# Sparse attention with a two-deep exp arena, context products issued one head pair late, and V passed through device memory

## The reference

```python
x = x + layernorm(attention(layernorm(x)))      # block-sparse, 64 blocks of 64 tokens
x = x + layernorm(ffn(layernorm(x)))            # silu(x Wg) * (x Wu), then Wd; hidden 3072
# attention: query block qb attends to key blocks
#   0 and 63 : all 64
#   1        : 0, 1, 2, 63         62 : 0, 61, 62, 63
#   others   : 0, qb-1, qb, qb+1, 63
# each: softmax(q k^T / 8) v
```

## Time and profile before

| | us |
|---|---|
| median of 3 runs | 2392.13 (2385.08 to 2399.96) |
| profiled execution, its own time | 2390.2 |
| span of its slowest core (core 1) | 2388.7 |
| spans of all cores | 2375.0 to 2388.7 |
| `_p2`, from PE's first score matmul to its last context matmul | 491.6 to 897.5 |

### The profile page before, as it was taken

One profiled execution on the slowest core, in us unless ns is written; L12 is line 12 of the kernel. 1 busy time (PEld: TensorE's weight loads), 2 busy tenths in 40 slices (PEclk: granted clock), 3 DMA queues, 4 the chain that ended last, 5 costly groups with the idle time before them and its releaser, 6 DMA issues.

```text
span 2388.7 us, 31359 instructions; the slowest of 8 cores (2375.0 to 2388.7 us)
## 1 busy us (share of the span) xinstructions
PE 1660.0 (69%) x11234; PEld 802.9 (34%) x11234; DVE 850.9 (36%) x2276; ACT 587.5 (25%) x794; POOL 339.1 (14%) x510
## 2 busy tenths in 40 slices
PE   0069999977777770000002989999999989999994
PEld 0024444444444440000001434444444434444442
DVE  3514343344444446466671111223122131223123
ACT  2421111155665441212222101112111111112121
POOL 2011212202111211000001202111111212121110
PEclk9999999977666765555556999999999999999997
DMA  9933323311112128985638717655656758665653
GB/s 230 276 93 71 82 60 89 123 47 63 55 55 87 33 45 177 206 186 135 151 106 163 75 19 71 120 57 91 86 57 120 71 107 78 117 60 99 78 66 104
DMA packets 359497, 239.33 MB, mean 100 GB/s; under 512 B 313008, under 2 KB 314672, under 8 KB 357296
## 3 DMA queue, kind: packets, MB, share of 16 engines
q0 software_dynamic: 225456, 111.33, 33.1%
q1 hardware_dynamic: 120064, 92.43, 15.7%
q10 hardware_dynamic: 13824, 33.56, 4.2%
HBM read 205.53 MB, written 75.63 MB: 118 GB/s over the span
## 4 chain that ended last, share of the span: by engine, by line
PE 43%; DVE 7%; DMA 6%; SPq 3%; ACT 2%; issue 1%; ACTq 1%; DVEq 0%; POOL 0%; POOLq 0%
PE gp L913 14%; PE upp L919 14%; PE yp L931 7%; DMA xn_d<-p_xn 4%; PE upp L931 3%; PE gp L931 3%; SPq L652 2%; DMA p_ctx<-ctxT_d 2%; DVE p_x L728 1%; DVE y_sb L993 1%; ACT p_xn L798 1%; DVE bst3b L734 1%; DVE bst3b L736 1%; SPq L888 1%; DVE p_attn L690 1%
## 5 line engine op out<-in xcount | busy, mean ns | idle before, releaser
L913 PE MATMUL gp<-x2T,wg_sb 128*128 128x512 bf16 x1536 | 376.3, 389 | 434.9 <-DMA x2T<-xn_d 398.9
L919 PE MATMUL upp<-x2T,wu_sl 128*128 128x512 bf16 x1536 | 368.4, 383 | 0.0
L913 PEld LDWEIGHTS gp<-x2T,wg_sb 128*128 128x128 bf16 x1536 | 152.2, 99 | 625.3 <-issue 451.6
L981 DVE TENSOR_TENSOR hswb<-upp,sgbuf 128x512 bf16<-128x512 f32 x192 | 132.8, 692 | 590.0 <-PE upp L919 590.0
L859 POOL DMA_DIRECT2D wu_sl<-wuT x192 | 168.1, 878 | 991.5 <-PE upp L919 611.7
L555 ACT ACTIVATE arenaB<-pp 128x768 bf16<-128x768 f32 (+2 forms) x312 | 232.3, 1086 | 148.7 <-PE pp L512 148.7
L958 ACT ACTIVATE sgbuf<-gp 128x512 bf16<-128x512 f32 x192 | 114.7, 597 | 574.3 <-PE gp L913 574.2
L919 PEld LDWEIGHTS upp<-x2T,wu_sl 128*128 128x128 bf16 x1536 | 152.2, 99 | 187.9 <-issue 11.5
L512 PE MATMUL pp<-qt_buf,kt_buf 64*64 64x64 bf16 (+2 forms) x3232 | 159.0, 313 | 74.7 <-ACT arenaB L555 61.1
L392 PE MATMUL qp<-xn1T,wq_sb 128*128 128x512 bf16 x512 | 122.6, 383 | 121.6 <-DMA xn1T<-xn_d 121.2
L931 PE MATMUL yp<-wd_sb,hswb 128*128 128x512 bf16 x768 | 197.1, 379 | 8.4 <-DVE hswb L981 8.4
(11 more groups left out here) (84 smaller groups left out, 1214.6 us busy)
## 6 DMA issues: line engine op xcount, KB each, us to landing
wu_sl<-wuT POOLq DMA_DIRECT2D x192, 256.0 KB, 4.5
xbuf<-x_in SPq DMA_DIRECT2D x32, 512.0 KB, 11.3
p_x<-x_in SPq DMA_DIRECT2D x32, 512.0 KB, 10.7
x_d<-p_x ACTq DMA_DIRECT2D x32, 512.0 KB, 6.8
x1f<-x_d SPq DMA_DIRECT2D x32, 512.0 KB, 5.0
out<-obuf POOLq DMA_DIRECT2D x32, 512.0 KB, 5.6
ctxT_d<-cstage POOLq DMA_DIRECT2D x128, 65.0 KB, 2.0
xn_d<-xn1buf ACTq DMA_DIRECT2D x32, 256.0 KB, 7.9
```

What stands on the lines that cost most here:

```text
L913: mm = te.matmul(gsl, wg_sb[:, dc * FF + hc * 128:dc * FF + (hc + 1) * 128], x2T[:, par * 8 * 512 + dc * 512:par * 8 * 512 + (dc + 1) * 51 ...
L919: mm = te.matmul(usl, wu_sl[:, (hc % 4) * 1024 + dc * 128: (hc % 4) * 1024 + (dc + 1) * 128], x2T[:, par * 8 * 512 + dc * 512:par * 8 * 51 ...
L981: v.tensor_tensor(hswb[:, hc * 512:(hc + 1) * 512], upp[:, (ghc % 2) * 512:(ghc % 2 + 1) * 512], sgbuf[:, (ghc % 2) * 512:(ghc % 2 + 1) * ...
```

## The change

- V no longer stays in SBUF. `v_sb` now lives only in `_p1b`, in memory that `_p1a` used; before its first write DVE waits until all writes of `xn1_d` have landed. At the end of `_p1b` POOL writes all of `v_sb` to a new device tensor `v_d` in one DMA (semaphore `s_vsp`).
- In `_p2` there are two arenas, `aru0` and `aru1`, used in turn by head pair. They lie over the memory of `v_sb`, so ACT waits for `s_vsp` before its first exp. SP waits for it too, then loads the V slice of each head pair into `vu_buf`, which holds two: 128 x 32 pieces of 130 values (260 bytes).
- PSUM is split: `psS` (4 banks, two group buffers, `par = gg % 2`) for the scores, `pc0` and `pc1` (2 banks each) for the context.
- PE's order becomes S(0) S(1) C(0) S(2) C(1) ... S(7) C(6) C(7) (`ctx_emit` is C). DVE's becomes the memsets of 0, then for each u the copies of C(u-1) followed by the memsets of u; the last turn has only the copies of C(7).

```diff
+    v_d = scratch("v_d", [128, 32 * 1040], BF16)
...
+              "s_ql0 s_ql1 s_vsp s_vl0 s_vl1 s_spe s_exp s_ms s_cpe s_cev0 s_cev1 "
               "s_cs00 s_cs01 s_cs10 s_cs11 "
...
     def _p1b():
-        v_sb = hold["v_sb"]
+        v_sb_cm = nc.sbuf_tensor("v_sb", [128, 32 * 1040], BF16)
+        v_sb = v_sb_cm.__enter__()
...
             def _(v):
+                v.wait_ge(sm.s_sp10, 16 * NT // 2)
+                v.wait_ge(sm.s_sp11, 16 * NT // 2)
                 v.memset(v_sb[:, 64:32 * 1040:65], 1.0).then_inc(sm.s_vev, 1)
...
+                g.wait_ge(sm.s_vev, 1 + V_COPY_TOTAL)
+                g.dma_start(v_d[:, :], v_sb[:]).then_inc(sm.s_vsp, 16)
...
     def _p2():
-        v_sb = hold["v_sb"]
...
-            nc.sbuf_tensor("arenaB", [128, 2 * A], BF16) as arenaB,
+            nc.sbuf_tensor("aru0", [128, 2 * A], BF16) as aru0,
+            nc.sbuf_tensor("aru1", [128, 2 * A], BF16) as aru1,
+            nc.sbuf_tensor("vu_buf", [128, 2 * 32 * 130], BF16) as vu_buf,
             nc.sbuf_tensor("cstage0", [65, 2 * 512], BF16) as cstage0,
             nc.sbuf_tensor("cstage1", [65, 2 * 512], BF16) as cstage1,
-            nc.psum_tensor("pp8", [128, 8 * 512], F32) as pp8,
+            nc.psum_tensor("psS", [128, 4 * 512], F32) as psS,
+            nc.psum_tensor("pc0", [128, 2 * 512], F32) as pc0,
+            nc.psum_tensor("pc1", [128, 2 * 512], F32) as pc1,
...
+            arus = (aru0, aru1)
...
             def _(sy):
-                for u in range(2, 8):
...
+                sy.wait_ge(sm.s_vsp, 16)
+                for u in range(8):
+                    if u >= 2:
+                        sy.wait_ge(sm.s_spe, SGROUPS * (u - 1))
...
+                        sy.dma_start(qt_buf[:, (u % 2) * S:(u % 2 + 1) * S],
+                                     qkt_d[0, u, :, :]).then_inc((sm.s_ql0, sm.s_ql1)[u % 2], 16)
+                        sy.dma_start(kt_buf[:, (u % 2) * S:(u % 2 + 1) * S],
+                                     qkt_d[1, u, :, :]).then_inc((sm.s_ql0, sm.s_ql1)[u % 2], 16)
+                    if u >= 2:
+                        sy.wait_ge(sm.s_cpe, 16 * (u - 1))
+                    sy.dma_start(
+                        vu_buf[:, (u % 2) * 4160:(u % 2 + 1) * 4160].rearrange(
+                            "p (s e) -> p s e", e=130),
+                        v_d[:].rearrange(
+                            "p (s e) -> p s e", e=1040)[:, :, 2 * u * 65:2 * u * 65 + 130]).then_inc(
+                        (sm.s_vl0, sm.s_vl1)[u % 2], 16)
...
+            def ctx_emit(te, u):
+                te.wait_ge(sm.s_exp, SGROUPS * (u + 1))
+                te.wait_ge(sm.s_ms, MS_INC_PER_U * (u + 1))
+                te.wait_ge((sm.s_vl0, sm.s_vl1)[u % 2], 16 * (u // 2 + 1))
...
+                        pc = (pc0, pc1)[h01]
+                        n_e = len(CTX_LISTS[C])
+                        for ei, (t, acol, pcol, w) in enumerate(CTX_LISTS[C]):
+                            mm = te.matmul(
+                                pc[0:65, (C % 2) * 512 + pcol:(C % 2) * 512 + pcol + w],
+                                vu_buf[:, (u % 2) * 4160 + t * 130 + h01 * 65:
+                                       (u % 2) * 4160 + t * 130 + h01 * 65 + 65],
+                                arus[u % 2][:, h01 * A + acol:h01 * A + acol + w],
+                                start=(ei == 0), stop=(ei == n_e - 1))
+                        mm.then_inc(sm.s_cpe, 1)
...
             def _(te):
-                last_use = {}
+                for u in range(9):
+                    if u < 8:
+                        up = (u % 2) * S
+                        te.wait_ge((sm.s_ql0, sm.s_ql1)[u % 2], 32 * (u // 2 + 1))
+                        for gi in range(SGROUPS):
+                            gg = u * SGROUPS + gi
+                            if gg >= 2:
+                                te.wait_ge(sm.s_exp, gg - 1)
+                            par = gg % 2
...
+                            last.then_inc(sm.s_spe, 1)
+                    if u >= 1:
+                        ctx_emit(te, u - 1)
+            @blk.scalar
+            def _(s):
+                s.wait_ge(sm.s_vsp, 16)
                 for u in range(8):
+                    if u >= 2:
+                        s.wait_ge(sm.s_cpe, 16 * (u - 1))
...
-                        par = gi % 4
-                        if par in last_use:
-                            te.wait_ge(sm.s_exp, last_use[par] + 1)
-                        last_use[par] = gg
...
-                    te.wait_ge(sm.s_exp, SGROUPS * (u + 1))
-                    te.wait_ge(sm.s_ms, MS_INC_PER_U * (u + 1))
...
-                                mm = te.matmul(
-                                    pp8[0:65, pcoff + pcol:pcoff + pcol + w],
-                                    v_sb[:, t * 1040 + h * 65: t * 1040 + h * 65 + 65],
-                                    arenaB[:, h01 * A + acol:h01 * A + acol + w],
-                                    start=(ei == 0), stop=(ei == n_e - 1))
-                            mm.then_inc(sm.s_cpe, 1)
...
+                        par = gg % 2
...
-                        src_ap = pp8[:, par * 1024:(par + 1) * 1024].rearrange(
+                        src_ap = psS[:, par * 1024:(par + 1) * 1024].rearrange(
...
-                        dst_ap = arenaB[:].rearrange("p (b c) -> p b c", b=2)[
+                        dst_ap = arus[u % 2][:].rearrange("p (b c) -> p b c", b=2)[
...
-                for u in range(8):
-                    for gi in range(SGROUPS):
-                        gg = u * SGROUPS + gi
-                        t = 0 if gi < 8 else gi - 7
...
-                        last.then_inc(sm.s_ms, 1)
-                    for C in range(NCH):
-                        v.wait_ge(sm.s_cpe, u * 16 + C * 2 + 1)
...
+                for u in range(9):
+                    if u >= 1:
+                        uu = u - 1
+                        for C in range(NCH):
+                            v.wait_ge(sm.s_cpe, uu * 16 + C * 2 + 1)
...
+                            v.tensor_copy(cstage0[:, (C % 2) * 512:(C % 2 + 1) * 512],
+                                          pc0[0:65, (C % 2) * 512:(C % 2 + 1) * 512]).then_inc(sm.s_cev0, 1)
+                            v.wait_ge(sm.s_cpe, uu * 16 + C * 2 + 2)
...
+                            v.tensor_copy(cstage1[:, (C % 2) * 512:(C % 2 + 1) * 512],
+                                          pc1[0:65, (C % 2) * 512:(C % 2 + 1) * 512]).then_inc(sm.s_cev1, 1)
+                    if u < 8:
+                        for gi in range(SGROUPS):
+                            gg = u * SGROUPS + gi
+                            t = 0 if gi < 8 else gi - 7
...
+                            v.wait_ge(sm.s_exp, gg + 1)
...
+                                    last = v.memset(
+                                        arus[u % 2][half * 64:half * 64 + 64,
+                                                    h01 * A + SEG_OFF[t] + lo:
+                                                    h01 * A + SEG_OFF[t] + hi], 0.0)
+                            last.then_inc(sm.s_ms, 1)
...
-        hold["v_sb"] = es_v.enter_context(
-            nc.sbuf_tensor("v_sb", [128, 32 * 1040], BF16, side="right"))
...
         _p1b()
+        hold["v_sb_cm"].__exit__(None, None, None)
```

More of the change, by code:

```diff
@@ L171, in build_nc @@
               "s_qsp0 s_qsp1 s_ksp0 s_ksp1 "
-              "s_ql0 s_ql1 s_spe s_exp s_ms s_cpe s_cev0 s_cev1 "
+              "s_ql0 s_ql1 s_vsp s_vl0 s_vl1 s_spe s_exp s_ms s_cpe s_cev0 s_cev1 "
               "s_cs00 s_cs01 s_cs10 s_cs11 "
@@ L303, in _p1b @@
     def _p1b():
-        v_sb = hold["v_sb"]
+        v_sb_cm = nc.sbuf_tensor("v_sb", [128, 32 * 1040], BF16)
+        v_sb = v_sb_cm.__enter__()
+        hold["v_sb_cm"] = v_sb_cm
         qstage = hold.get("qstage")
@@ L486, in _ @@
             @blk.tensor
             def _(te):
-                last_use = {}
-                for u in range(8):
-                    up = (u % 2) * S
-                    te.wait_ge((sm.s_ql0, sm.s_ql1)[u % 2], 32 * (u // 2 + 1))
-                    if u >= 1:
-                        te.wait_ge(sm.s_cev0, 8 * u)
-                        te.wait_ge(sm.s_cev1, 8 * u)
+                for u in range(9):
[8 more added lines that the diff above has]
+                            t = 0 if gi < 8 else gi - 7
+                            jt, jb = PAIRS[t]
+                            runs = [(8 * gi, 8)] if t == 0 else pair_runs(t)
+                            col = 0
+                            last = None
+                            for (qs, n) in runs:
+                                w = n * 64
+                                for (rows, hoff) in ((0, 0), (64, 512)):
+                                    rhs = qt_buf[rows:rows + 64,
+                                                 up + qs * 64: up + qs * 64 + w]
+                                    for (tcol, j) in ((0, jt), (64, jb)):
+                                        last = te.matmul(
```

(52 more changed lines are left out.)

66 lines of the change are left out of this document (14 added, 52 removed).

## The result

| | before | after |
|---|---|---|
| median, us | 2392.56 (2385.08 to 2399.96, 10 runs) | 2440.39 (10 runs, lowest 2434.8) |
| ratio | 1 | 1.0199, 95% interval 1.0182 to 1.0217 |
| profiled execution, us | 2390.2 | 2467.09 |

What follows compares the result with a forecast made beforehand. In the attention stage ACT and PE take turns, neither full. The wait for V (+25.1) and the joints, loop and tail together (+17.7) sum to +42.8 on 2390.2: 2433 us, range 2405 to 2465.

Steps and rivals of the forecast that it cites:

- Step 1: Attention joints: ACT's idle time per turn becomes C - 0.15 in place of C + 2.7, six turns in place of seven.
- hole: PE idle for 15 us ahead of C(7), while DVE does the last head pair's memsets.
- Step 2: Scores with two group buffers: small groups share a 1.60 us loop, so an S takes 32.0 us, 3.0 more each.
- Step 3: End of attention: memsets of head pair 7 stand behind C(6)'s copies, so C(7) starts 15.4 us after C(6) ends.
- Step 4: Start of attention: ACT's first exp waits for the V write's landing while PE does two groups; +25.1 us.
- rival B: V write before attention runs at 204 GB/s: +18.8 us, giving 2452; chance 0.12.
- Step 5: V slice loads, SP's queue order and DVE's wait for `xn1_d` cost nothing; slices land within 18 us.
- A: Score loop: exps hand over early enough that two buffers suffice, 24 us less, giving 2409; chance 0.13.
- C: Score loop is longer, at the recorded exp length: 35 us more, giving 2468; chance 0.11.
- D: Attention not slower: vanished joints keep PE at the high clock, small group perhaps 0.35 us, giving 2398; chance 0.05.

Runs made afterwards that it cites:

- Experiment 5: Changed kernel with V written in nine pieces, memsets ahead of copies, three score group buffers, one context bank per head, against the kernel before: ratio 0.9954.
- experiment 1: Kernel before with two score group buffers in place of four: ratio 1.0105, +25.1 us; with three: 0.9981.
- experiment 4: Changed kernel with DVE's memsets of head pair u moved ahead of the copies of C(u-1): ratio 1.0140 to the kernel before, 14.1 us below the change.
- Experiment 2: Kernel before plus one unused write of V to device memory at the end of `_p1b`: ratio 1.0126 issued by POOL, 1.0013 by SP.
- e_write_pool: Kernel before plus one unused write of V to device memory, issued by POOL: both times 2418.4 us; its repeat gave ratio 1.0126.
- experiment 6: Changed kernel with matmuls of C(u-1) spread between score groups of S(u): ratio 0.976 to the kernel before; with V also written in nine pieces: 0.9625.

## Why the prediction was right

**Step 1, the joints.** Right. Forecast: all turns together shrink by 20.9 us. Read on core 3: what lies between the exps of one S and the next falls from 147.8 us to 128.3, so 19.4 saved. ACT's six idle times are 16.5 to 20.9 us, each 0.1 to 0.5 less than the C in it, where "C - 0.15" was forecast. Experiment 5 bears it out as a whole: it has the joints saved, no loop and no hole, and its stretch from the first exp to C(7) is 16.7 us shorter than before, with a C that is 1.0 us longer. Its gain of 11.0 us (6.7 to 15.1) is less than that because it still waits 10.0 us at the barrier, where the kernel before waits 3.1.

**Step 2, the loop.** Right, in each number: loop 1.60 forecast, 1.60 read; S 32.0 forecast, 32.1 to 32.5 read by its exps; +24 forecast, +25.1 measured by itself in experiment 1, and +25.6 by the exps of the changed kernel on core 3 (257.9 us in eight S, 232.3 before).

**Step 3, the tail.** Right: 15.4 forecast, 15.77 read, 14.1 by experiment 4. The sum of 1 to 3 was +17.7 and came out at +21.9 on core 3 (+23.3 as the mean of cores 0 to 3, 379.35 to 402.65). On core 3 the 4.2 us too much are all accounted for. 1.5 are the base: the core of the earlier trace rows has 381.6, core 3 has 380.1. The rest is 402.0 against the 399.3 of the forecast: eight S of 32.24 in the mean (+1.9), 0.3 between S(0) and S(1), six turns (+1.1) and the tail (+0.4), less 0.9 for a C(6) that was shorter than the mean.

**Step 4, the wait for V.** The size held, the mechanism did not. Forecast +25.1, measured +27.5 to the first exp, of it 0.5 for a V copy that ended later. The size held because the forecast's wait and the real one last as long as the same transfer; that is luck as far as the mechanism goes. The landing was taken as 25 and was 24.8 on the page and 25.5 on core 3, so 8.52 MB went at about 340 GB/s, next to the 334 of ACT's queue and far from the 204 of rival B. Of the Trainium skill's two rules that stood beside it, "DMA: Bandwidth & Descriptors", Specifications (25.8), agrees with this row, and the setup-cost fit of "SBUF — State Buffer" (21.5) lies 3 to 4 us below it. But the step that ACT stands behind the landing while PE does two groups was wrong. The barrier stands behind it, through POOL's drain, so PE began nothing, and from the landing (493.77 + 25.5 = 519.3) to the first exp were 3.3 us in place of the 1.4 of the forecast: the end of the drain, the barrier and the first matmuls came in between. Experiment 2 shows what this means for whoever changes the kernel: by the forecast's mechanism it would have helped to move ACT's wait or the arena, but e_write_pool has neither and pays the same; the queue or the time of the write had to change.

**Step 5, at nothing.** Right for the V slices, by the changed kernel's answer on their line (core 3; the columns are the issue's lengths, the stretch of issue times, and the idle time that they ended):

```profile
L490 SPq DMA_DIRECT2D vu_buf<-v_d x8: 524/524/3676, 520.4 to 859.4; - x8
```

They landed in 7.1 to 12.6 us, median 8.5, against the 18 taken as the most, and nobody waited. A C was 18.6 us in the mean both before and after (core 3, 16.8 to 21.0 after). DVE's new wait for `xn1_d` showed no cost: the memset behind it starts at 131.8 on core 3, and DVE's first Q work is at 144.7.

**The rivals.** A fell in experiment 1 and B by the 25.5 us. C fell by the loop: the exp hands over as the unqueued one does. D's condition did not come about (clock 0.50 to 0.60 in every S), but its price for a small group was right: experiment 6 has the clock at 0.96 with the pieces and 0.89 to 0.91 without, and the small group then took 0.36 us, where D had put 0.35.

The whole, by runs: +30 for the write by POOL, +25 for the loop, +14 for the tail; 47.6 leaves -21 for the joints, and -20.9 was forecast. That agreement is better than the intervals (8, 5 and 8.5 us to each side) allow one to claim; the trace's 19.4 is the firmer number.
